# Products of zeros behind each step of a recurrent kernel on TensorE

## The reference

```python
x = x + hyperbolic_block(x, cond[:, None, :], ...)   # 16 heads of 16, feed-forward width 1024
x = x + lstm(x, cond, Wx, Wh, b)

def lstm(x, h0, Wx, Wh, b):
    xW = einsum('ntd,dk->tnk', x, Wx) + b
    def step(carry, xw_t):
        prev_h, prev_c = carry
        a = xw_t + prev_h @ Wh
        i, f, o, g = sigmoid(a[:, :H]), sigmoid(a[:, H:2*H]), sigmoid(a[:, 2*H:3*H]), tanh(a[:, 3*H:])
        next_c = f * prev_c + i * g
        next_h = o * tanh(next_c)
        return (next_h, next_c), next_h
```

## Time and profile before

| | us |
|---|---|
| median of 3 runs | 1952.37 (1934.43 to 1959.62) |
| the profiled execution | 1961.72 |
| its span, first to last instruction | 1959.8 |
| TensorE busy with products | 1387.5 (71%) |
| VectorE busy | 1161.9 (59%) |
| ScalarE busy | 909.3 (46%) |
| GpSimd busy | 553.0 (28%) |
| gate products L693, 16384 of them | busy 525.4, TensorE idle before them 339.8 |

### The profile page before, as it was taken

The page is one execution under the profiler, slowest core; times in us unless marked ns, Lnnn a source line. Parts: engine busy times, 40 slices in busy tenths (PEclk is TensorE's granted clock), DMA queues, the critical chain, the costliest instruction groups (busy, mean ns, idle before and its releaser), DMA issues.

```text
span 1959.8 us, 60022 instructions
## 1 busy us (share of the span) xinstructions
PE 1387.5 (71%) x22071; PEld 1191.0 (61%) x22071; DVE 1161.9 (59%) x6482; ACT 909.3 (46%) x3335; POOL 553.0 (28%) x1726
## 2 busy tenths in 40 slices
PE   3656576248788878787878787878776857576764
PEld 3544454137676767676767676767665756565653
DVE  5455565006676767666656576666655565656555
ACT  0333376116565656554545465545443343333333
POOL 4222214330433333323333333232324040313100
PEclk9676755555555565555555555555555555555555
DMA  7000000000000000000000000000000000000000
GB/s 215 0 0 0 0 1 2 0 3 3 2 8 2 8 2 8 2 8 2 8 2 8 2 8 2 8 2 8 2 7 3 7 6 4 5 2 5 2 5 5
DMA packets 16689, 18.00 MB, mean 9 GB/s; under 512 B 6036, under 2 KB 15384, under 8 KB 16408
## 3 DMA queue, kind: packets, MB, share of 16 engines
q1 hardware_dynamic: 13016, 10.51, 1.9%
q10 hardware_dynamic: 3392, 3.81, 0.7%
HBM read 12.21 MB, written 2.10 MB: 7 GB/s over the span
## 4 chain that ended last, share of the span: by engine, by line
PE 47%; DVE 13%; POOL 11%; issue 9%; ACT 7%; POOLq 1%; DVEq 0%; ACTq 0%
PE psum L693 17%; PE psum L637 6%; PE psum L669 6%; PE psum L645 6%; POOL sc L244 4%; PE psum L683 3%; DVE cnew L1154 3%; ACT ot L903 2%; DVE hl L1163 2%; PE psum L653 2%; PE psum L575 2%; DVE hl L1161 2%; DVE gO L1149 2%; ACT weights L799 1%; PE psum L620 1%
## 5 line engine op out<-in xcount | busy, mean ns | idle before, releaser
L693 PE MATMUL psum<-hl,wh 128*128 128x8 f16 x16384 | 525.4, 172 | 339.8 <-DVE hl L1163 339.7
L693 PEld LDWEIGHTS psum<-hl,wh 128*128 128x128 f16 x16384 | 505.8, 104 | 422.8 <-DVE hl L1163 402.4
L897 ACT ACTIVATE tA<-gA 128x16 f32<-128x16 f32 x512 | 110.1, 215 | 550.2 <-DVE gA L1145 548.1
L1145 DVE TENSOR_REDUCE gA<-psum 128x16 f32<-128x32 f32 x512 | 96.7, 189 | 278.5 <-PE psum L693 275.8
L292 POOL TENSOR_SCALAR sc<-sc 128x1 f32<-128x1 f32 x97 | 23.1, 238 | 795.7 <-DVE sc L1122 362.6
L244 POOL TENSOR_TENSOR sc<-sc,cst 128x1 f32<-128x1 f32 (+1 forms) x260 | 198.8, 765 | 48.0 <-POOL sc L292 18.1
L1051 DVE TENSOR_TENSOR weights<-w,weights 128x256 f16<-128x256 f32 x512 | 203.7, 418 | 13.5 <-ACT weights L799 12.7
L575 PE MATMUL psum<-qTs,kT 64*128 64x128 f16 x1024 | 152.4, 301 | 6.7 <-ACT weights L799 3.7
L805 ACT ACTIVATE w<-psum 128x512 f32<-128x512 f32 x256 | 154.6, 604 | 0.2
L799 ACT ACTIVATE weights<-psum 128x512 f16<-128x512 f32 x256 | 153.3, 599 | 0.0
L903 ACT ACTIVATE ot<-cnew 128x8 f32<-128x8 f32 x512 | 109.5, 214 | 85.3 <-DVE cnew L1154 39.9
(11 more groups left out here) (230 smaller groups left out, 2302.1 us busy)
## 6 DMA issues: line engine op xcount, KB each, us to landing
arena<-in_x_dram SPq DMA_DIRECT2D x4, 512.0 KB, 9.7
wf<-in_L_cond_w_f_dram SPq DMA_DIRECT2D x2, 1024.0 KB, 17.4
xr<-in_x_dram SPq DMA_DIRECT2D x64, 32.0 KB, 1.7
out_dram<-place SPq DMA_DIRECT2D x64, 32.0 KB, 1.6
qTs<-in_L_cond_w_ada_dram ACTq DMA_DIRECT2D x1, 1536.0 KB
oT<-in_L_cond_Wh_dram ACTq DMA_DIRECT2D x1, 1024.0 KB, 14.2
wx<-in_L_cond_Wx_dram SPq DMA_DIRECT2D x1, 1024.0 KB, 19.0
rows<-in_L_cond_b_ada_dram ACTq DMA_DIRECT2D x4, 128.0 KB, 14.7
```

The source lines that it names most:

```text
L693: last = mm(cols, wh16[:, half, kc, (g0 + c) * P:(g0 + c + 1) * P], hl[:, :, kc, :, 2].rearrange("p e b -> p b e"), start=False, stop=c == ...
```

## The change

`keep_busy` is called for each slot from FIRST to T - 2, also before t = 0. A new function `streamed` counts the columns that TensorE streams in a slot: 256 for the gate products, 264 and 512 for the two parts of a head, 2048 for a first, second or input product and for a round of gate inputs (counted in the slot before it), 3072 for r = 0, 256 for each pair of transposes. If the count is under 2048, products of zeros with D = 256 columns are added until it comes to at least 3000 (LIGHT), else until it comes to 3600 (HEAVY). Before t = 0 the goal is 1300 (EARLY) in slots with a head and 0 in others. The products multiply `zeros` (128x256, float16) with `ident16` and add to the free half of pF; they wait until VectorE has read this step's gF from the same bank, where before they would have waited for gO and used pO.

```diff
-FILL = False
+LIGHT, HEAVY, EARLY = 3000, 3600, 1300
...
+            def streamed(t):
+
+                cols = 256 * (t >= 0) + 264 * (t - 5 in HEAD_AT) + 512 * (t in HEAD_AT) + 256 * (t % RING == 1 and t > RING)
+                cols += 2048 * (t >= 0 and (t + 1) % ROUND == 0)
+                for k in range(NT):
+                    cols += 256 * (t - merged_slot(k) == 8)
+                for r in ((t + PAUSE) % RING, (t + PAUSE) % RING + RING):
+                    if r < PAUSE and 0 <= (t + PAUSE - r) // RING < NT:
+                        cols += 3072 * (r == 0) + 256 * (r in (24, 41)) + 2048 * (25 <= r < 33 or 42 <= r < 46)
+                return cols
+
             def keep_busy(t):
 
-                left = 1.0
...
-                count = int(left / 0.11)
-                if count > 0:
-                    pe.wait_ge(s["l_gO"], t + 1)
-                    for i in range(count):
-                        mm(pO[:, D:2 * D], ident16[:], zeros[:], start=False, stop=False, skip_group_check=True)
+                cols = streamed(t)
+                wanted = LIGHT if cols < 2048 else HEAVY
+                if t < 0:
+                    wanted = EARLY if t in HEAD_AT else 0
+                count = max(0, -((cols - wanted) // D))
+                if count > 0 and t >= 0:
+                    pe.wait_ge(s["l_gF"], t + 1)
+                for i in range(count):
+                    mm(pF[:, D:2 * D], ident16[:], zeros[:], start=False, stop=False, skip_group_check=True)
...
-                if FILL and 0 <= t < T - 1:
+                if t < T - 1:
                     keep_busy(t)
```

More of the change, by code:

```diff
@@ L712, in out_rows @@
                 last.then_inc(s["o_T"], 1)
-            def keep_busy(t):
-                left = 1.0
[L717 to L721, removed]
-                count = int(left / 0.11)
-                if count > 0:
-                    pe.wait_ge(s["l_gO"], t + 1)
-                    for i in range(count):
-                        mm(pO[:, D:2 * D], ident16[:], zeros[:], start=False, stop=False, skip_group_check=True)
+            def streamed(t):
[7 more added lines that the diff above has]
+                return cols
+            def keep_busy(t):
+                cols = streamed(t)
[7 more added lines that the diff above has]
+                    mm(pF[:, D:2 * D], ident16[:], zeros[:], start=False, stop=False, skip_group_check=True)
             for t in range(FIRST, T):
```

## The result

The changed kernel takes 1880.28 us (median of 4, 1876.28 to 1883.32); the kernel before, run beside it, 1955.99. The ratio is 0.9647, 95% interval 0.9564 to 0.973: 3.5% faster. The forecast was 1876, 76 us less than before; the measured difference is 76. The profiled execution took 1876.28 us with a span of 1874.4, against 1961.72 and 1959.8.

What follows compares the result with a forecast made beforehand. Light steps were taken as bound by a three-engine chain, dense ones by TensorE's low clock. Terms -38.5 (blocks without heads), -44.2 (with heads), 0 (first two blocks), +2 (early heads), +5 (light steps) gave -76: 1876 us, range 1828 to 1985.

Steps and rivals of the forecast that it cites:

- What bounds the kernel, and that zeros would move it: Recurrence: light steps bound by a three-engine chain, dense ones by TensorE at 1.2 GHz; zeros lift the clock, 76 us less.
- The dense four with heads: Second layer, norm, gate inputs and output product in blocks with heads: 20.7 us falls to 14.5 at the upper clock.
- Price of a product of zeros: One product of 128 rows and 256 columns on TensorE: 0.11 us at the upper clock, 0.21 at the lower.
- The half microsecond: Objection from the skill's page: at about 81 ns per 128 columns, an empty step would last some 0.5 us more.
- Empty steps: Steps with only gate products: eleven fast zeros issued by 2.27 us, next gates at 2.33, so cost 0.
- the second rival: Clock falls at the wait for X or after dense steps, light steps can't lift it; chance 0.11 for over 2% slower.
- A block with heads: 32 steps with attention heads, from 98.9 us: faster dense, first-layer and input steps, less slow light steps, gain 8.0 us.
- The allowance of 2.0 us for slow light steps after a fall: In each block with heads, light steps paying for zeros at the lower clock after it falls: +2.0 us.
- The wait for X, with heads: Step waiting for X plus input product in blocks with heads: clock falls in the gap, yet 1.3 us gained.
- The first 64 steps: First two blocks: 12 us gained each in dense steps, against some 25 slow light steps at 0.9 us: net 0.
- Early heads: Attention heads before t = 0: three slow zeros add 0.3 us each until the clock rises; +2 us, bounds 0 and 18.
- The premise about scores on 64 rows: Scores load 64 of 128 rows, so the first 64 steps, all with a head, are weaker at lifting the clock.

Runs made afterwards that it cites:

- light_3600: Changed kernel with the light steps' goal raised from 3000 to 3600 columns, three more products of zeros each: 1885.72 us.
- before_x_free: Changed kernel plus 14 products of zeros ahead of each wait for X, into a bank nobody reads then, without waiting for gF: 1857.76 us.
- heavy_only: Changed kernel without zeros in light steps; dense steps and slots before t = 0 keep theirs: 1909.05 us.
- no_early: Changed kernel without the zeros before t = 0 (EARLY = 0): 1855.67 us.
- half_rows: Changed kernel with each product of zeros on 64 rows instead of 128, same columns and count: 2470.56 us.
- best3: Changed kernel, EARLY 0, no zeros in steps 0 to 8, goal 3600 to step 63 then 3000, 14 zeros ahead of waits for X in a free bank: 1808.95 us.

## Why the prediction was right, point by point

**What bounds the kernel, and that zeros would move it:** right. The dense four with heads take 13.5 us (883.1 to 896.6) against 20.7 and 14.5 predicted; without heads 12.7 against 18.4 and 13.0 predicted; the first layer 9.9 and 10.6 against 10.0 and 10.8 predicted. All are at the upper level.

**Price of a product of zeros:** 0.11 us fast was right: eleven fit between 1.06 and the gates at 2.32 us, and three more lengthened the step by 0.28, as 3 x 0.11 less the slack. So was 0.21 slow (nine in 2.10 us). The half microsecond that the prediction worked out from the section Back-to-back issue gap of the Trainium skill's page "TensorE: Matmul & The Clock Gate" did not come. Its doubling of a figure for 128 columns to one for 256 was the prediction's own step; at 128 columns themselves four fast scores take 0.39 us, less one latency of 0.227 some 0.054 from one to the next. The section has about 81 ns there, and the trace does not agree.

**Empty steps:** cost 0, right; the 5 us put in for them were not paid.

**The clock:** it held through light steps in every block from step 64 on, which the second rival doubted. That light steps at the lower level don't lift it by themselves held at this goal of columns; with three more zeros (light_3600, one execution) they did, in step 4. A block with heads was forecast to gain 8.0 us and gained 9.9 (850.7 to 939.7). The allowance of 2.0 us for slow light steps after a fall was not needed: the clock was at its lower level only in the wait for X and the input steps behind it.

```profile
918.50:928.70 10.20, 9.00 (x104) 7.51 (x105) 6.21 (x35) 4.80 (x18) 3.33 (x12) 0.50 0.01 2
```

Over eight blocks 1.9 us each is 15 of the 17 us by which the second stretch gained more than forecast (61.2, not 44.2). The third gained 43.7 and not 38.5: at three of its five waits for X, as in the block shown, the clock did not fall (4.7 us, clock 1.00) and all four input steps were fast.

**The wait for X, with heads:** the fall and the slow zeros were foreseen, but priced too cheap. Step and input product took 6.1 and 12.6 us after (916.2 to 934.9), 18.7 together, against some 18.5 before: -1.3 was predicted, nothing came. before_x_free shows what is lost there.

**The first 64 steps:** predicted 0, measured -1.5. The gain in dense steps and the price of slow light steps with a head nearly cancel, as said; heavy_only shows the latter to be about 13 us.

**Early heads:** this step failed: 2 us were predicted, with 18 as the upper bound, and 21 were measured (24.6 by no_early). The prediction had three zeros lengthen a head's turn from 1.0 to 1.3 us, and only until the clock rises. It never rose there: it stayed at the lower level from 256.3 us to beyond the last early head at 352, with TensorE 94% busy from 256 to 266. The turn was too short as well, 1.52 us measured; part of that was absorbed where TensorE had waited between groups of heads before. The premise about scores on 64 rows, applied to the first LSTM steps, was not applied here. half_rows shows that rows used matter; that the scores are what keeps the early stretch down is argued from it and not tried alone.

Against the profiled execution, the early heads were 19 us worse than forecast and all the rest 29 us better: 17 in the second stretch, 5 in the third, 1.5 in the first, and the 5 put in for light steps. That makes 85, not 76. The medians differ by 76 only because the two profiled executions lie on opposite sides of their medians. So the exact hit is luck, twice over; the mechanism, a clock held by zeros that fit behind the gates, was right, and so were its signs: empty steps 2.32 apart, the dense step at 3.77 to 3.81 us, the clock 0.94 and 1.00 over a block.

## What to carry to other kernels

Products of zeros pay where dense work on TensorE is separated by a latency chain that leaves it idle, provided that they all end before the chain does: enough to hold the clock or none, since 3 fewer a step cost 45 us here. Don't put them into stretches where they fail to lift the clock, there they are a plain delay (21 us before the recurrence). Put them where the gap is: ahead of an in-order wait and behind no semaphore that is signalled only after that wait.

## What the runs showed of the hardware that was not expected

Products of zeros on 64 of 128 rows, as many as those on 128 and as long at the lower level, left the mean granted clock of the whole span at 0.534 and the kernel at 2470.56 us, against 0.858 and 1880.28. A busy TensorE alone does not keep the clock up: in best3 it fell at 1190.8 us though TensorE was busy all of the 3.40 us before. The gate products (8 columns) run at the same pace at either level: 32 of them in 1.01 to 1.05 us.
